# A decoder's last mixture of experts: finished rows scattered straight to the output, its table's zeros and its masks moved to GpSimd

## The reference

```
xf = rmsnorm(h)                              # 2048 rows of 128
vals, idx = top_k(xf @ router_w + router_b, 2); scores = softmax(vals)
emask = one_hot(idx) * (cumsum(...) < cap)   # an expert takes rows only up to a capacity
m = max over the two choices of the expert kept
y = (gelu((xf @ w2[m]) * (xf @ w1[m]))) @ w3[m]          # 128 -> 256 -> 128
out = h + sum over the two choices of score * (y if kept else xf)
```

## Time and profile before

| | |
|---|---|
| median of 3 runs | 1675.45 us (1674.0 to 1679.46) |
| the profiled execution | 1675.38 us, span 1673.6 us |
| TensorE busy | 1423.6 us (85% of the span) |
| VectorE busy | 966.6 us (58%) |
| ScalarE busy | 749.0 us (45%) |
| GpSimd busy | 232.3 us (14%) |
| chain that ended last | TensorE 69%, VectorE 15%, issue 4%, SyncE's queue 4%, DMA 3% |
| mean granted clock of TensorE | 0.922 |

### The profile page before, as it was taken

One profiled execution on the slowest core, in us unless ns is written; L12 is line 12 of the kernel. 1 busy time (PEld: TensorE's weight loads), 2 busy tenths in 40 slices (PEclk: granted clock), 3 DMA queues, 4 the chain that ended last, 5 costly groups with the idle time before them and its releaser, 6 DMA issues.

```text
span 1673.6 us, 43831 instructions
## 1 busy us (share of the span) xinstructions
PE 1423.6 (85%) x17681; PEld 878.2 (52%) x17681; DVE 966.6 (58%) x2541; ACT 749.0 (45%) x1927; POOL 232.3 (14%) x201
## 2 busy tenths in 40 slices
PE   4889888696499999999958999889989898999672
PEld 3343434393266666766633466346644564456462
DVE  4354635323477777777723676576665776477532
ACT  1323142251266666666613276327723672447431
POOL 1011120123030030200010200030002100120124
PEclk7989999797799999999978899999989998899897
DMA  9600000023230100100021000000000000000012
GB/s 327 264 17 1 17 1 7 17 58 98 77 140 4 26 19 10 35 4 16 4 76 43 1 2 2 5 7 2 2 5 7 2 2 1 7 1 1 6 55 70
DMA packets 62072, 60.07 MB, mean 36 GB/s; under 512 B 27952, under 2 KB 47024, under 8 KB 60720
## 3 DMA queue, kind: packets, MB, share of 16 engines
q1 hardware_dynamic: 59536, 53.04, 10.0%
q0 software_dynamic: 2048, 4.20, 0.9%
q10 hardware_dynamic: 288, 0.03, 0.0%
HBM read 32.73 MB, written 24.51 MB: 34 GB/s over the span
## 4 chain that ended last, share of the span: by engine, by line
PE 69%; DVE 15%; issue 4%; SPq 4%; DMA 3%; ACT 3%; POOL 2%; ACTq 0%; POOLq 0%; DVEq 0%
PE ps L1126 7%; PE ps L1514 6%; PE ps L1533 5%; PE ps L500 5%; PE ps L1547 4%; PE ps L1106 4%; PE ps L1116 4%; DVE arena L586 4%; PE ps L1147 4%; PE ps L258 4%; PE ps L1502 3%; PE ps L474 3%; PE ps L1161 2%; PE ps L1556 2%; PE ps L797 2%
## 5 line engine op out<-in xcount | busy, mean ns | idle before, releaser
L1259 DVE TENSOR_REDUCE nmax<-ps 128x1 f32<-128x512 f32 x256 | 166.8, 683 | 56.3 <-PE ps L1116 55.7
L1590 ACT ACTIVATE arena<-ps,arena 128x512 f32<-128x512 f32 (+3 forms) x256 | 135.5, 531 | 119.1 <-DVE arena L1650 112.9
L1650 DVE TENSOR_REDUCE arena<-ps 128x1 f32<-128x512 f32 (+3 forms) x256 | 124.3, 487 | 78.8 <-PE ps L1518 76.7
L1219 ACT ACTIVATE arena<-ps,nmax 128x512 f32<-128x512 f32 x172 | 119.0, 692 | 80.8 <-DVE nmax L1259 79.3
L1533 PE MATMUL ps<-sqc,arena 128*128 128x128 f32 x640 | 106.6, 287 | 20.0 <-DVE arena L1658 19.7
L586 DVE TENSOR_REDUCE arena<-ps 128x8 f32<-128x1232 f32 x64 | 89.2, 1438 | 40.3 <-PE ps L462 40.1
L258 PE MATMUL ps<-identb 128*128 128x512 bf16 x408 | 110.0, 430 | 1.4 <-DVE kcol L707 1.4
L1267 DVE COPY arena<-ps 128x512 f32<-128x512 f32 x128 | 88.0, 688 | 39.9 <-PE ps L1126 38.4
L1514 PE MATMUL ps<-arena 64*128 64x384 f32 (+3 forms) x512 | 106.2, 493 | 0.0
L1658 DVE TENSOR_SCALAR arena<-arena 128x512 f32<-128x512 f32 (+3 forms) x256 | 100.8, 394 | 9.1
L598 DVE RECIPROCAL arena<-ps 128x128 f32<-128x128 f32 x8 | 7.7, 959 | 160.4 <-PE ps L500 160.4
(11 more groups left out here) (350 smaller groups left out, 2713.1 us busy)
## 6 DMA issues: line engine op xcount, KB each, us to landing
xs_d<-onehot SPq DMA_DIRECT2D x3, 3072.0 KB, 29.6
cw<-in_cw SPq DMA_DIRECT2D x2, 2048.0 KB, 13.4
rv<-in_rv SPq DMA_DIRECT2D x2, 1536.0 KB, 19.7
late<-in_gw SPq DMA_DIRECT2D x3, 1024.0 KB, 10.8
arena<-xs_d SPq DMA_DIRECT2D x46, 64.0 KB, 1.8
xs_d<-arena SPq DMA_DIRECT2D x46, 64.0 KB, 1.6
xs_d<-onehot SPq DMA_DIRECT2D x1, 2560.0 KB, 22.4
onehot<-q_s SPq DMA_DIRECT2D x96, 8.0 KB
```

Of the source, the lines that this page charges most:

```text
L1219: nc.scalar.activation(PB[k % 6], ps[:, k % 5, :], ACT.Exp, bias=nmax[:, u:u + 1], accum_out=rsum[:, b % 2, u:u + 1]).then_inc(SD["exp"], 1)
L1259: nc.vector.tensor_reduce(nmax[:, k % NU:k % NU + 1], ps[:, k % 5, :], AX.X, ALU.max, negate=True)\
L1590: nc.scalar.activation(TF["p%d" % (n % 2)][:, h * S:h * S + wd], ps[:, FSB[n % 2][h], 0:wd], ACT.Exp, bias=TF["nmax"][:, k4:k4 + 1], accum ...
L1650: nc.vector.tensor_reduce(TF["nmax"][:, k4:k4 + 1], ps[:, FSB[n % 2][h], 0:wd], AX.X, ALU.max, negate=True)\
```

## The change

1. **A table of its own for G.** `gs_d` has rows of 258 floats: the normalised row (128), xo (128), cy, and the row's output index less 2 * 2048. The four are kept side by side in `G4`, in the memory of C's expert weights, which are one tensor `cw` now. `pool_G_send` sends whole rows of `G4`. A zero row's index, with 2 * 2048 added, is past the end of the output.
2. **The zeros of that table** are written by GpSimd in four plain DMAs from its own queue (`pool_G_zero`), between expand(0) and spread(2) of D. GpSimd waits for them before the first send. REGION shrinks from 2560 to 17 * 128 rows for both tables; `rows4` is capped at the table's end.
3. **No stores and no gathers.** VectorE's last instruction of a tile is cy * y + xo out of PSUM and the loaded row; GpSimd adds 2 * 2048 to the loaded indices and scatters the 128 finished rows to the output, dropping rows whose index is past its end. SyncE only loads. The final gathers, adds and stores are gone.
4. **Weights.** ScalarE copies the up-projections in place of GpSimd, two tiles ahead, into three buffers.
5. **Masks.** `dve_prepare`'s casts move to GpSimd (`pool_prepare`), ahead of its work on `selw`. The small column `pcol` stays on VectorE, in the first batch of B.
6. Three small VectorE instructions that write the indices into `G4`, after D.

```diff
-REGION = 2560
+REGION = 17 * P
+GROWS = E1 * REGION + P
@@ masks
+        def pool_prepare(pool):
+            pool.wait_ge(s_const[1], 16 * len(GROUPS[1]))
+            nc.gpsimd.tensor_copy(xmask[:, :, 0:KP], xmask_in)
+            nc.gpsimd.tensor_copy(xmask[:, :, KP:KW], xmask_in[:, :, 0:KW - KP])
+            for mask, given in ((amask, amask_in), (kmask, kmask_in)):
+                nc.gpsimd.memset(mask[:, :, KS:KP], MASKED)
+                nc.gpsimd.tensor_scalar(mask[:, :, 0:KS], given[:, :, :], MASKED, None, ALU.mult)
+                ins = nc.gpsimd.tensor_scalar(mask[:, :, KP:KW], given[:, :, 0:KW - KP], MASKED, None, ALU.mult)
+            ins.then_inc(s_mask, 1)
+            nc.gpsimd.tensor_copy(cpick[:, :, :], causal_in[:, 0:2, :])
+            nc.gpsimd.tensor_copy(cmask[:, :, :], causal_in[:, 2:4, :]).then_inc(s_mask, 1)
@@ pool_D
             expand(0)
+            pool_G_zero(pool)
             for b in range(2, B):
@@ G's rows
+        GW4 = 2 * P + 2
+        G4 = cw[:, 0:NTT * GW4].rearrange("p (t n) -> p t n", n=GW4)
+        gs_d = nc.dram_tensor("gs_d", (GROWS, GW4), F32, kind="Internal").ap()
@@ pool_G_send
-                nc.gpsimd.indirect_dma_start(xs_d, ..., yn4(b)[:, n, :], None).then_inc(SC["sent"], 16)
+            if b == 0:
+                pool.wait_ge(SG["zero"], 16 * 4)
+                nc.gpsimd.indirect_dma_start(gs_d, ..., G4[:, n, :], None).then_inc(SC["sent"], 16)
@@ act_G
+            def weights(s):
+                e = act.value_load(expert4[0:1, s:s + 1], min_val=0, max_val=E2 - 1)
+                if s >= 3:
+                    act.wait_ge(SC["h"], NS + s - 2)
+                nc.scalar.copy(TG[f"w{s % 3}"]..., gw12[:, :, bass.ds(e, 1), :]...).then_inc(SC["w1"], 1)
+            act.wait_ge(SG["table"], 1)
+            weights(0)
+            weights(1)
             linear(0)
             for s in range(NS):
+                if s + 2 < NS:
+                    weights(s + 2)
@@ dve_G
                 if s >= 4:
-                    dve.wait_ge(SC_st[s % 4], 16 * (st_c[s % 4] + s // 4))
-                V.tensor_copy(TG[f"y{s % 4}"], ps[:, 6 + s % 2, 0:P]).then_inc(SC["yb"], 1)
-            ... (the adds of cy * y, L1926)
+                    dve.wait_ge(SG_out[s % 4], 16 * (s // 4))
+                V.scalar_tensor_tensor(TG[f"y{s % 4}"], ps[:, 6 + s % 2, 0:P], XBG[s % NXB][:, 2 * P:2 * P + 1],
+                                       XBG[s % NXB][:, P:2 * P], ALU.mult, ALU.add).then_inc(SC["yb"], 1)
@@ sp_G
+            for s in range(NS):
+                r = sp.value_load(rows4[0:1, s:s + 1], min_val=0, max_val=GROWS - P)
                 if s >= NXB:
-                    sp.wait_ge(SC["tx"], NS + s - NXB + 1)
+                    sp.wait_ge(SC["yb"], NS + s - NXB + 1)
+                    sp.wait_ge(SG["idx"], s - NXB + 1)
+                sp.dma_start(XBG[s % NXB], gs_d[bass.ds(r, P), :]).then_inc(SC_ld[s % NXB], 16)
-            ... (the stores of result tiles, L1945)
+        def pool_G_zero(pool):
+            zero = kmask[:, :, :].rearrange("p b n -> p (b n)").bitcast(F32)[:, 0:GW4]
+            nc.gpsimd.memset(zero, 0.0).then_inc(s_own, 1)
+            pool.wait_ge(s_own, 2)
+            rows = gs_d.rearrange("(p r) d -> p r d", p=P)
+            for z in range(4):
+                r0, r1 = z * (GROWS // P) // 4, (z + 1) * (GROWS // P) // 4
+                nc.gpsimd.dma_start(rows[:, r0:r1, :], zero.unsqueeze(1).to_broadcast([P, r1 - r0, GW4])).then_inc(SG["zero"], 16)
@@ pool_G
-            ... (the weight copies, L1955, and the gathers, L1960)
+            for s in range(NS):
+                pool.wait_ge(SC_ld[s % NXB], 16 * (ld_c[s % NXB] + s // NXB + 1))
+                if s >= 4:
+                    pool.wait_ge(SG_out[s % 4], 16 * (s // 4))
+                nc.gpsimd.tensor_scalar(gidx[:, s % 4:s % 4 + 1], XBG[s % NXB][:, 2 * P + 1:GW4], 2.0 * B * S, None, ALU.add)\
+                    .then_inc(SG["idx"], 1)
+                pool.wait_ge(SG["idx"], s + 1)
+                pool.wait_ge(SC["yb"], NS + s + 1)
+                nc.gpsimd.indirect_dma_start(out_rows, bass.IndirectOffsetOnAxis(ap=gidx[:, s % 4:s % 4 + 1], axis=0),
+                                             TG[f"y{s % 4}"], None, bounds_check=B * S - 1, oob_is_err=False)\
+                    .then_inc(SG_out[s % 4], 16)
```

More of the change, by code:

```diff
@@ L189, in decoder @@
         s_prep = sem("s_prep")
+        s_mask = sem("s_mask")
         s_zero = sem("s_zero")
@@ L856, in dve_tiles @@
             ch(V.scalar_tensor_tensor(s_row[:, :], s_e[:, :], float(REGION), s_t[:, :], ALU.mult, ALU.add))
-            V.tensor_copy(rows4[:, :], s_row[:, :]).then_inc(done, 1)
+            V.tensor_scalar(rows4[:, :], s_row[:, :], float(limit), None, ALU.min).then_inc(done, 1)
         def dve_C(dve, ch):
@@ L1686, in pool_F @@
                     .then_inc(SF["qr"], 1)
-        SG = {n: sem("s_g_" + n) for n in ("gate", "d", "e2", "oh", "cum", "seen", "pick", "rank", "slot", "count", "table", "a", "p")}
+        SG = {n: sem("s_g_" + n) for n in ("gate", "d", "e2", "oh", "cum", "seen", "pick", "rank", "slot", "count", "table", "a", "p", "zero", "idx")}
+        SG_out = [sem("s_g_out%d" % i) for i in range(4)]
         ld_c, st_c = ([len(range(z, NS, n)) for z in range(n)] for n in (NXB, 4))
@@ L1827, in pool_G_send @@
             pool.wait_ge(SG["slot"], b + 1)
-            for n in range(NT):
-                nc.gpsimd.indirect_dma_start(xs_d, bass.IndirectOffsetOnAxis(ap=slot4[:, b * NT + n:b * NT + n + 1], axis=0),
-                                             yn4(b)[:, n, :], None).then_inc(SC["sent"], 16)
+            if b == 0:
+                pool.wait_ge(SG["zero"], 16 * 4)
+            for n in range(b * NT, b * NT + NT):
+                nc.gpsimd.indirect_dma_start(gs_d, bass.IndirectOffsetOnAxis(ap=slot4[:, n:n + 1], axis=0),
+                                             G4[:, n, :], None).then_inc(SC["sent"], 16)
         def pe_G(pe):
@@ L1932, in sp_G @@
             sp.wait_ge(SG["table"], 1)
-            def load(s):
-                r = sp.value_load(rows4[0:1, s:s + 1], min_val=0, max_val=XROWS - P)
+            for s in range(NS):
+                r = sp.value_load(rows4[0:1, s:s + 1], min_val=0, max_val=GROWS - P)
                 if s >= NXB:
-                    sp.wait_ge(SC["tx"], NS + s - NXB + 1)
-                sp.dma_start(XBG[s % NXB], xs_d[bass.ds(r, P), :]).then_inc(SC_ld[s % NXB], 16)
-            for s in range(NXB):
-                load(s)
@@ L2045, in _ @@
             sp_G(sp)
-            for b in range(B):
-                sp.wait_ge(s_xout, b + 1)
-                sp.dma_start(out[b:b + 1].rearrange("o (t p) d -> p (o t) d", p=P), xo4(b)).then_inc(s_store, 16)
-            sp.wait_ge(s_store, B * 16)
         @block.tensor
@@ L2135, in _ @@
             ch.turn(0)
+            ch(nc.vector.tensor_reduce(g_p[:, 0:1], c["tri"], AX.X, ALU.add))
+            ch(nc.vector.tensor_scalar(g_p[:, 0:1], g_p[:, 0:1], -1.0, float(P - 2 * B * S), ALU.mult, ALU.add))
+            ch(nc.vector.tensor_scalar(G4[:, :, 2 * P + 1], row["index"][:, 0:NTT], float(P), g_p[:, 0:1], ALU.mult, ALU.add))
             for b in range(B):
```

86 lines of the change are left out of this document (30 added, 56 removed).

## The result

The changed kernel is slower: 1699.5 us (median of four) beside 1674.7, ratio 1.0133, 95% interval 1.0067 to 1.0199; a second measurement of the same kernel (below, k_again) gave 1.0073, 1.0040 to 1.0107. I had said 1644 and at most 1690.

| stage | marker, before to after (us) | forecast | measured |
|---|---|---|---|
| head | GpSimd's masked keys of the second batch, 101.23 to 92.37 | -4.5 | -8.9 |
| to the first expansion | 554.49 to 544.51 | 0 | -1.1 |
| relative attention | first to second expansion, 99.24 to 145.80 | 0 | **+46.6** |
| to the last send | 930.63 to 920.11 long | 0 | -10.5 |
| first result | last send to first result, 15.15 to 16.48 | +0.5 | +1.3 |

What follows compares the result with a forecast made beforehand. SyncE's load queue was taken to pace the last loop, with one serial chain as the tail. 1675.4 - 24.85 (tail) - 2.95 (loop) + 0.5 (rows) - 4.5 (head) = 1643.6 us, said 1644; forecast's range 1638 to 1656, overall 1638 to 1690.

Steps and rivals of the forecast that it cites:

- Relative attention: GpSimd's four zero writes, 18.1 MB, between its first and third batch's work: no stall taken, 0 us.
- have 28 us to spare: SyncE's third-batch loads sharing the DMA engines with the zeros: 28 us slack, beyond which each microsecond costs one.
- The sign that I had named: Third batch's first scores at about 636; over 2 us later, with GpSimd's build ending just before, means hold exceeded cover.
- The pace: Zero writes' queue paced by data at the head's 352 GB/s: 51 us, the middle of three estimates, under the cover.
- the bounds that I gave: GpSimd's hold by the zero writes: 4 us from four issues, up to 134 us at 7.7 ns a row.
- my cover of 69.4: Relative attention: GpSimd may be held 69.4 us, until 627.8, before its third-batch build delays TensorE at 641.
- the rules that I weighed: Skill pages on the zero writes: many descriptors emitted before visible cost; 1032 B rows drain slower, 64 us for 51.
- The rival "held too long": Zero writes hold GpSimd past 69.4 us, up to 134 at 7.7 ns a row, 1709 us; slower 0.15, same 0.05, part gain 0.14.
- Tail: After the last tile only one scatter follows, 3.1 us instead of 27.95: gain 24.85 us, lower bound 23.
- Loop: Last mixture's loop: ScalarE sets 1.95 us a tile, 42.9 us against 45.85: gain 2.95; ends gain 7.6, loss 9.
- Head: Mask work moved from VectorE to GpSimd at the start: gain 4.5 us, ends 4.7 and 0.
- Longer rows: Sends and loads of 1032 B rows for 512 B, only the first of each exposed: +0.5 us, ends 0 and 1.8.

Runs made afterwards that it cites:

- k_again: The changed kernel run once more, unchanged, to see its spread: 1684.4 us (1681.7 to 1694.0), ratio 1.0073.
- c_late_D: Changed kernel with three of four zero writes after GpSimd's last relative-attention build, the fourth in the later cross-attention layer: 1682.4 us, ratio 1.0034.
- l_dose: Changed kernel with one of four zero writes (4.5 MB) left in the relative attention, the other three in the later cross-attention: 1663.1 us, ratio 0.9919.
- i_hold77: Changed kernel with zero writes moved to the later cross-attention; 132 GpSimd memsets, 77 us without DMA traffic, in their old place: 1663.2 us, ratio 0.9942.
- f_head: The kernel before with only the masks moved to GpSimd and the column work moved behind them: 1668.5 us, ratio 0.9965.

## Why the prediction was wrong, step by step

*Relative attention, the step that failed.* I wrote "I take no stall, since the pace of the data is the middle of the three and lies under the cover", and that SyncE's loads "have 28 us to spare". I asked what the 18 MB do to GpSimd and to SyncE, the two engines that issue something there, and not what they do to the DMA engines' other users. TensorE uses them as well: its instructions come in packets through queue q8, one for some 250 instructions, and in this layer it needs one in 4.7 us. With the engines full it got one in 8.7. So the step put the traffic's own cost at nothing; it measured 46.6 us, 31.1 of them standing and 15.5 slower matmuls at the lower clock that came with the waits. The traffic without hold or loads cost 36 us for 13.5 MB (c_late_D), in proportion (l_dose) the same. The sign that I had named came out accordingly: the third batch's first scores stood at 677.59, where I had about 636, but GpSimd's build had ended 10.75 us before them, so the hold was not what they waited for.

The pace failed too: I took the head's 352 GB/s, 51 us. The rows of 1032 B went at 181 GB/s, over 99.9 us. That GpSimd was held 70 us, 77 us with the issues, is inside the bounds that I gave (4 to 134 us), and 10 us of stall followed from such a hold in i_hold77, for 8 by my cover of 69.4. Had TensorE not been slowed, the late build (ready at 666.84, where 641 less the head's 8.9 was due) would by that sum have cost some 35 us by itself, which no run shows; the two lay beside each other, and in the changed kernel TensorE met no wait for the build.

On the rules that I weighed: the Trainium skill, "DMA: Bandwidth & Descriptors" (Anatomy of one DMA, SWDGE path), has many descriptors emitted before their cost shows. The trace agrees for three issues of 1.8 us and ends at the fourth, with its 69.92 us. The same page (How a descriptor splits into AXI transactions) made 64 us of the 51; measured were 99.9, so it pointed the right way and fell short. The user that I missed stands in the Trainium skill, "Runtime: NRT & Kernel Launch" (Instruction fetch mechanics): instructions come in 16 KiB blocks of 256 over a DMA queue of the sequencer's own, and crossing a block is mostly hidden. The size agrees (16.4 KB, and waits 256 matmuls and weight loads apart). "Mostly hidden" holds in the kernel before, with waits of 0.44 and 0.93 us at two such places in that stretch, and not beside a bulk write.

*The rival "held too long"* named a slower kernel at this place, with 0.34 in all and 0.15 of it for slower, but by the wrong mechanism: its price per row would have shown TensorE waiting for GpSimd at the third batch.

*Tail.* 9.3 us for 3.1. The step "What follows the last tile is one scatter" failed: GpSimd was two scatters behind (4.6 us until the last one starts, where I had 0.28), and from its start to the end it took 4.7 us, where I had 2.24 from a chain that ended in another wait, and 0.3. The lag is the term that I priced at 1.46 to 1.74 us a tile: its own semaphore came back in 0.80, not 0.28.

*Loop.* 43.75 us for 42.9, right in the number, by luck: it was not ScalarE's 1.87 us. ScalarE is busy 0.37 + 0.62 + 0.41 = 1.40 and stands 0.28 for the register read, where I had 0.43. TensorE's matmuls and ScalarE's copy wait for each other, and no one engine is full (TensorE is busy 37.6 of the 43.75 us).

*Head.* The step was right (4.7 in f_head, 4.5 forecast); the other 4 us in the changed kernel lie beside a higher clock, and their cause stays open.

*Longer rows.* +1.3 for +0.5, within the ends of 0 and 1.8.

*The range.* The forecast's upper end, 1656, holds the loop's end alone: with the head at 0 and the rows at 1.8 as well, the ends add up to 1661. And it said that a measurement tells 5 us from no change, where the two measurements of the changed kernel lie 15 us apart.

## What to carry to other kernels

Before a bulk transfer is put beside busy engines, list every user of the DMA engines there, the instruction queue among them: its packets in the window against what the engine with most instructions per microsecond needs. Put bulk writes where that number is low (here a stretch with 5.4 matmuls per us lost nothing, one with about 26 lost 2.1 to 2.7 us a MB), and try larger pieces: 3096 B cost less than half of what 1032 B did; nothing larger was run. A wait named "issue" is checked by counting: if the engine's waits stand a packet's instructions apart, it waited for instructions. When a chain of small steps paces a queue, take its own semaphore out of the step, by doing the first part a tile or two ahead.

## What had not been expected of the hardware

- One instruction packet of 16.4 KB serves 256 matmuls and weight loads, the step between TensorE's waits, and with the DMA engines 86% taken by a GpSimd bulk write one arrived in 8.7 us instead of 4.7. Where in between a packet waits is open: a packet's own time on an engine grew only from 1.1 us (1.5% of 16 engines over 104 us, 22 packets) to 1.4.
- A bulk write from GpSimd ran at 181 GB/s in pieces of 1032 B (204 in k_again) and at 342 GB/s in pieces of 3096 B, which took 55% of the engine time for the same bytes.
- GpSimd's queue took three writes of 4.5 MB in 1032 B pieces and held the engine 70 us before the fourth; in 3096 B pieces it took all five at once.
- GpSimd's own semaphore costs it 0.80 us behind a one-column add, and 0.30 behind a memset of 258 columns (548.29 + 0.31 to 548.91).
